# One core, sixteen batches: set-up loads in another order, batch 0's condition rows and the weight products in the score banks, waits at the first user, and a new order table

## What is computed

```python
ada = t_emb @ w_ada + b_ada                      # 16 rows of 1536; t_emb is cond_1024
sh_msa, sc_msa, g_msa, sh_mlp, sc_mlp, g_mlp = jnp.split(ada, 6, axis=-1)
xn = layer_norm(logmap0(x)); xm = expmap0(xn * (1 + sc_msa) + sh_msa)
q, k, v = heads(plin(xm, w_q, b_q)), ...         # 16 heads of 16
attn = softmax(qt @ kt / 4); attn_out = plin(from_heads(attn @ vt), w_o, b_o)
x = mobius_add(x, expmap0(g_msa * logmap0(attn_out)))
xm = expmap0(layer_norm(logmap0(x)) * (1 + sc_mlp) + sh_mlp)
ff = plin(plin(xm, w_f1, b_f1), w_f2, b_f2)      # no nonlinearity between the two
h = mobius_add(x, expmap0(g_mlp * logmap0(ff)))
y = x_in + attn_block(h)     # windows of 64, 64 latents, two sigmoid gates, w_out
out = y + moe(modulated(y, cond, weight))        # softmax, top 2 of 4, relu(x Wi + B A x) Wo
```

## Time and profile before

| | us |
|---|---|
| median of 3 runs | 1327.85 (1326.16 to 1328.44) |
| profiled execution | 1326.44 |
| its span | 1324.6 |
| TensorE busy | 1181.0 |
| VectorE busy | 906.8 |
| ScalarE busy | 711.2 |
| GpSimd busy | 214.9 |

### The profile page before, as it was taken

The page is one execution under the profiler, slowest core; times in us unless marked ns, Lnnn a source line. Parts: engine busy times, 40 slices in busy tenths (PEclk is TensorE's granted clock), DMA queues, the critical chain, the costliest instruction groups (busy, mean ns, idle before and its releaser), DMA issues.

```text
span 1324.6 us, 34251 instructions
## 1 busy us (share of the span) xinstructions
PE 1181.0 (89%) x13940; PEld 826.7 (62%) x13940; DVE 906.8 (68%) x3547; ACT 711.2 (54%) x1460; POOL 214.9 (16%) x176
## 2 busy tenths in 40 slices
PE   3867778989999999999999999999999989888776
PEld 1444445656666676767777676767676766666555
DVE  4557877877777797779777877697877784342412
ACT  0256676655567664575557655756575463333221
POOL 0301103012030220213021301122011220101101
PEclk8888898989999999999999999999999999999888
DMA  9210010001001010100000000000000000000000
GB/s 317 73 64 13 18 29 26 9 26 38 2 16 47 10 41 11 42 10 31 21 26 18 18 26 22 22 3 29 2 30 15 18 15 18 10 10 18 2 9 8
DMA packets 26974, 38.55 MB, mean 29 GB/s; under 512 B 3472, under 2 KB 21264, under 8 KB 26816
## 3 DMA queue, kind: packets, MB, share of 16 engines
q1 hardware_dynamic: 25472, 34.79, 8.3%
q10 hardware_dynamic: 1344, 1.57, 0.4%
HBM read 31.67 MB, written 4.29 MB: 27 GB/s over the span
## 4 chain that ended last, share of the span: by engine, by line
PE 68%; DVE 15%; ACT 12%; issue 3%; DMA 1%; POOL 0%; SPq 0%; DVEq 0%; POOLq 0%; ACTq 0%
PE psg L434 42%; PE psq L434 14%; PE pso L434 6%; PE psg L437 6%; ACT PQ L1337 6%; DVE TU L893 2%; DVE nm L896 1%; ACT QK L1337 1%; DVE ST L890 1%; DMA QK<-in_w_ada 1%; ACT M L1337 1%; ACT L1337 1%; DVE smf L890 1%; ACT JA L1348 1%; ACT OT L1340 1%
## 5 line engine op out<-in xcount | busy, mean ns | idle before, releaser
L1337 ACT ACTIVATE PQ<-psq 128x1280 f32<-128x1280 f32 (+2 forms) x144 | 215.5, 1496 | 102.2 <-PE psq L434 101.4
L1686 POOL TENSOR_TENSOR R<-R,rhoT 128x512 f32<-128x512 f32 x64 | 82.7, 1292 | 522.6 <-ACT R L1337 522.1
L434 PE MATMUL psg<-zT,WiT 128*128 128x256 f32 x512 | 126.0, 390 | 1.3 <-DVE R L893 1.3
L434 PE MATMUL pso<-PQ,Vg 128*32 128x256 f32 (+2 forms) x2048 | 116.8, 347 | 8.6 <-ACT PQ L1337 8.6
L434 PE MATMUL psq<-QK 32*128 32x128 f32 (+4 forms) x3328 | 123.2, 304 | 0.0
L434 PE MATMUL psg<-WoT,R 128*128 128x256 f32 x512 | 113.6, 379 | 0.0
L896 DVE TENSOR_REDUCE nm<-psq 128x16 f32<-128x2048 f32 (+1 forms) x48 | 92.8, 1933 | 26.1 <-PE psq L434 26.0
L434 PEld LDWEIGHTS psg<-zT,WiT 128*128 128x128 f32 x512 | 94.5, 194 | 16.5 <-issue 2.7
L434 PEld LDWEIGHTS psq<-QK 32*128 32x128 f32 (+1 forms) x3328 | 94.2, 166 | 16.4 <-issue 7.7
L434 PEld LDWEIGHTS psg<-WoT,R 128*128 128x128 f32 x512 | 95.9, 190 | 13.0 <-issue 0.5
L434 PE MATMUL psg<-wqkv,M 128*128 128x512 f32 (+1 forms) x256 | 97.8, 511 | 0.8 <-DVE ST L890 0.8
(11 more groups left out here) (223 smaller groups left out, 2360.3 us busy)
## 6 DMA issues: line engine op xcount, KB each, us to landing
bcA<-ada_rows SPq DMA_DIRECT2D x16, 384.0 KB, 3.4
...
QK<-NMT SPq DMA_DIRECT2D x128, 3.0 KB
...
```

Of the source, the lines that this page charges most:

```text
L434: return e.matmul(o, lhsT, rhs, start=start, stop=stop, skip_group_check=True)
L1337: return e.activation(o, i, func, **kw)
L1686: e.tensor_tensor(R4, R4, rhoT[:, :].unsqueeze(1).broadcast_to([128, 2, 256]), ALU.mult).then_inc(*pool_moe.mark(b, f"r{f}"))
```

## The change

The set-up loads come in another order: `w_ada` in four pieces, first those for columns 0 to 767, then the identity and `wqkv`, then the rest. The condition, both biases and `bqkv` are issued by ScalarE. One half of `w_ada` moves from `QK2` to `R2`, so that `w1T1` and `w21` no longer wait for the condition products. For batch 0 TensorE makes the first 768 condition values in all 128 partitions at once (the condition column broadcast as the stationary operand), VectorE adds the bias, which was loaded to 128 partitions, and writes `bcA[0]`. No DMA is in that path any more. The other rows go through the scratch as before. The weight products use banks 0 and 1 of `psq` instead of two `psg` banks, and are cut into pieces of two matmuls that the table places. Waits for loads that all stood in one place (`setup`, the end of `late`) stand at the first user. The norm factors are made for batch 0 alone, then 1 and 2, then 3. The table `ORDER` is new for all engines and over the whole program; a line of it is shown.

```diff
--- before
+++ after
@@ ORDER: the table of letters, one string of stages for each engine
-        "**n*qqqq**nhqhqqaqaaaan*aaaooohhoqaqqaaqaaaanaooohhoqaqqaaqaaaaaNooFFohhoaaaaaaaaooppppppomommnmNqqqFFql",
+        "AA*AAn*qqqq*******hhn**qqqqaanaaaaaaooohhqqqqaoaaaaaaanooohhqqqqaoaaaaaaNaooFFohhoaaaaaaaaooppppppnomqqq",
...
@@ where loads and signals are declared
-        wada = ST1.rearrange("p j n -> p (j n)"), QK2[0].rearrange("p e n -> p (e n)")[:, 0:1536]
+        wada = ST1.rearrange("p j n -> p (j n)"), R2.rearrange("p f n -> p (f n)")[:, 0:1536]
-        badaR = U[0][0:16, 0:768], U[1][0:16, 0:768]
+        bada = U[0][:, 0:768], U[1][0:16, 0:768]
-        pool_setup = sig("pool_setup", "ident", "identb", "zero", "ones")
+        pool_setup = sig("pool_setup", "zero", "ones", "ident", "identb")
-        quad = Banks([psq], dve_late.at(0, "ada3"))
-        po, pg = Banks([pso]), Banks(psg)
+        quad = Banks([psq], dve_ada.at(0, "a3"))
+        po, pg = Banks([pso], dve_ada.at(0, "a5")), Banks(psg)
-        units = [([0, 1], []), ([2, 3], []), ([], [0])]
+        units = [([0], []), ([1, 2], []), ([3], []), ([], [0])]
@@ TensorE
-            def setup():
+            def first(b, *names):
+                if not b:
+                    for k in names:
+                        w.wait_ge(*loads[k])
+            def ada(_):
+                yield
                 w.wait_ge(*loads["cond"])
                 for c in range(2):
-                    w.wait_ge(*loads[f"wada{c}"])
-                for j in range(3):
+                    w.wait_ge(*loads[f"wada{c}0"])
+                for j, n in ((0, 512), (1, 256)):
                     for c in range(2):
-                        last = mm(psq[0:16, j, :], condT[:, c, :], wada[c][:, 512 * j:512 * j + 512], c == 0, c == 1)
-                    last.then_inc(*pe_setup.mark(0, f"ada{j}"))
-                w.wait_ge(*pool_setup.at(0, "ones"))
-                for k in ("wqkv", "wo"):
-                    w.wait_ge(*loads[k])
+                        last = mm(psq[:, j, 0:n], condT[:, c, 0:1].broadcast_to([128, 128]), wada[c][:, 512 * j:512 * j + n],
+                                  c == 0, c == 1)
+                last.then_inc(*pe_ada.mark(0, "bc"))
+                for j, o in enumerate((psq[0:16, 2, :], psq[0:16, 3, :], pso[0:16, :])):
+                    yield
+                    if j:
+                        for c in range(2):
+                            w.wait_ge(*loads[f"wada{c}1"])
+                    for c in range(2):
+                        last = mm(o, condT[:, c, :], wada[c][:, 512 * j:512 * j + 512], c == 0, c == 1)
+                    last.then_inc(*pe_ada.mark(0, f"r{j}"))
             def late(_):
                 for ic in range(2):
-                    yield
-                    bank = take(pg, ("W", ic), act_late.at(0, f"W{ic}"))
-                    for k in ("w1T0", "w1T1", "w20", "w21"):
-                        w.wait_ge(*loads[k])
                     for f in range(8):
+                        if f % 2 == 0:
+                            yield
+                        if f == 0:
+                            w.wait_ge(*dve_ada.at(0, "c2"))
+                        w.wait_ge(*loads[f"w1T{f // 4}"])
+                        w.wait_ge(*loads[f"w2{f // 4}"])
                         v = wx[f // 4][:, f % 4, :]
-                        last = mm(bank[:, :], v[:, 128 * ic:128 * ic + 128], v, f == 0, f == 7)
+                        last = mm(psq[:, ic, :], v[:, 128 * ic:128 * ic + 128], v, f == 0, f == 7)
                     last.then_inc(*pe_late.mark(0, f"W{ic}"))
                 yield
                 bank = take(pg, ("b1w",), act_late.at(0, "b1x"))
...
-                yield
-                for k in ("wr", "wout", "w2c", "wrt", "wat0", "wat1", "wgkv", "WiT", "WoT"):
-                    w.wait_ge(*loads[k])
-                w.wait_ge(*dve_late.at(0, "Bst"))
-                w.wait_ge(*pool_late.at(0, "wgkv"))
-                w.wait_ge(*act_late.at(0, "b1b"))
...
+                    w.wait_ge(*pool_setup.at(0, "identb"))
+                    first(b, "wqkv")
+                        w.wait_ge(*act_late.at(0, "W1"))
+                first(b, "wo")
+                first(b, "wat0", "wat1")
+                        first(b, "WiT", "WoT")
...
@@ VectorE
+            def ada(_):
+                s = dve_ada
+                yield
+                w.wait_ge(*loads["bada0"])
+                w.wait_ge(*pe_ada.at(0, "bc"))
+                for k, i in enumerate((psq[:, 0, 0:256], psq[:, 0, 256:512], psq[:, 1, 0:256])):
+                    stt(bcA[0][:, k, :], i, float(k == 1), bada[0][:, 256 * k:256 * k + 256], ALU.add,
+                        ALU.add)().then_inc(*s.mark(0, f"c{k}"))
+                w.wait_ge(*loads["bada1"])
+                for j, i in enumerate((psq[0:16, 2, :], psq[0:16, 3, :], pso[0:16, :])):
+                    yield
+                    w.wait_ge(*pe_ada.at(0, f"r{j}"))
+                    for h in range(2):
+                        n, o = 2 * j + h, slice(256 * h, 256 * h + 256)
+                        k = 256 * (n % 3)
+                        stt(adaR[j][:, o], i[:, o], float(n in (1, 4)), bada[n // 3][0:16, k:k + 256], ALU.add,
+                            ALU.add)().then_inc(*s.mark(0, f"a{n}"))
             def late(_):
                 s = dve_late
...
-                yield
-                after(s)
-                for n, o in enumerate((adaR[0][:, 256:512], adaR[2][:, 0:256])):
-                    e.tensor_scalar(o, o, 1.0, None, ALU.add).then_inc(*s.mark(0, f"one{n}"))
                 yield
...
@@ ScalarE, the set-up
-                load(e, "bqkv", bqkv[:, :], A["bqkv"].partition_broadcast(128))
-                load(e, "bo", bo[:, :], A["b_o"].partition_broadcast(128))
+                load(e, "cond", condT[:, :, :], A["condT"].rearrange("(c p) b -> p c b", p=128))
+                load(e, "bada0", bada[0], A["b_ada"][0:768].partition_broadcast(128))
                 load(e, "w1T0", wx[0][:, :, 0:256], chunks("w1T")[:, 0:4])
                 load(e, "w20", wx[0][:, :, 256:512], chunks("w2")[:, 0:4])
+                load(e, "bqkv", bqkv[:, :], A["bqkv"].partition_broadcast(128))
+                load(e, "bada1", bada[1], A["b_ada"][768:1536].partition_broadcast(16))
+                load(e, "bo", bo[:, :], A["b_o"].partition_broadcast(128))
@@ GpSimd
-                return modulate(pool_norm, b, M1, bcA_in[b % 3].at(b // 3), bcA[b % 3], act_norm.at(b, "x1"))
+                rows_in = bcA_in[b % 3].at(b // 3 - (b % 3 == 0)) if b else dve_ada.at(0, "c2")
+                return modulate(pool_norm, b, M1, rows_in, bcA[b % 3], act_norm.at(b, "x1"))
@@ SyncE
-                load(e, "cond", condT[:, :, :], A["condT"].rearrange("(c p) b -> p c b", p=128))
                 for c in range(2):
-                    load(e, f"wada{c}", wada[c], chunks("w_ada")[:, c])
-                load(e, "bada0", badaR[0], A["b_ada"][0:768].partition_broadcast(16))
-                load(e, "bada1", badaR[1], A["b_ada"][768:1536].partition_broadcast(16))
+                    load(e, f"wada{c}0", wada[c][:, 0:768], chunks("w_ada")[:, c, 0:768])
+                load(e, "ident", ident0, A["ident"])
+                load(e, "wqkv", wqkv[:, :, :], chunks("wqkv"))
+                for c in range(2):
+                    load(e, f"wada{c}1", wada[c][:, 768:1536], chunks("w_ada")[:, c, 768:1536])
                 for _ in x_load(1):
                     pass
-                load(e, "ident", ident0, A["ident"])
-                load(e, "wqkv", wqkv[:, :, :], chunks("wqkv"))
-                load(e, "hsel", hsel[:, :], A["hsel"])
-                load(e, "wo", wo[:, :, :], chunks("w_o"))
-                for b in range(2, 4):
-                    for _ in x_load(b):
-                        pass
-                load(e, "b1c", b1c, A["b1c"])
-            def late(_):
-                chunks = lambda k: A[k].rearrange("(c p) n -> p c n", p=128)
-                yield
-                w.wait_ge(*pe_setup.at(0, "ada2"))
                 load(e, "w1T1", wx[1][:, :, 0:256], chunks("w1T")[:, 4:8])
                 load(e, "w21", wx[1][:, :, 256:512], chunks("w2")[:, 4:8])
-                yield
-                w.wait_ge(*dve_late.at(0, "one1"))
-                for j in range(3):
-                    e.dma_start(scratch[:, 512 * j:512 * j + 512], adaR[j]).then_inc(loads["ada"][0], 16)
+                load(e, "hsel", hsel[:, :], A["hsel"])
+                for _ in x_load(2):
+                    pass
+                load(e, "wo", wo[:, :, :], chunks("w_o"))
+                load(e, "b1c", b1c, A["b1c"])
+                for _ in x_load(3):
+                    pass
...
+            def ada(_):
+                for j, k in enumerate("AAB"):
+                    yield
+                    w.wait_ge(*dve_ada.at(0, f"a{2 * j + 1}"))
+                    e.dma_start(scratch[:, 512 * j:512 * j + 512], adaR[j]).then_inc(*loads[f"ada{k}"])
```

(6 more changed lines are left out.)

196 lines of the change are left out of this document (109 added, 87 removed).

## The result

The changed kernel takes 1293.7 us (median of 4 runs, 1292.49 to 1297.26) against 1327.01 (4 runs, 1326.06 to 1328.44) beside it. The ratio is 0.9753, 95% interval 0.973 to 0.9775, so it is 29.9 to 35.8 us faster. The forecast was 1293, and its range 1272 to 1318. The profiled execution took 1293.05 us, its span is 1291.3.

A forecast was written before the change was run, and what follows sets the result against it. TensorE was taken as the bound, busy 753.2 of 775 us mid-kernel, with gains only where it idles at the ends. Terms 14.7 + 2 + 0 + 10 + 8 off 1326.4 gave 1291.7, median 1293 us, range 1272 to 1318.

The forecast's parts named there:

- The start, term 14.7: Up to the first scores: these come at about 57 us in place of 71.7, 14.7 us earlier.
- Steps 1 to 6: Start, from first loads through weight products: batch 0's qkv at about 24.5 us in place of 49.97, products done at 47.3.
- the 10.5 of shared DMA engines: Start: condition values begin at 10.5 us if queues share DMA engines; separate queues would bring their 1 MB at 5 us.
- The two thin slacks: Start: heads ready at 42 to 44 us against 47, batch 1's condition values modulated at 44 against 48.
- step 7: End of the start: heads and transposes 1.3 us, bias and condition products 2.8, batch 1's qkv 5.3; first scores about 57.
- The early batches, term 2: From 71.7 to 157.7 us: 2 us gained, between -4 and +6.
- period of 28.8 us: Early batches: time from one attention output to the next, 28.8 us in place of 30.6.
- The middle, term 0: From 157.7 to 1075 us: no gain from the new order, between -15 and +15 us.
- The rival that the middle pays: From 300 to 1075 us: 0.45 us lost on each of 95 exponentials, 43 us more, 1336 us; chance 0.07.
- The tail, terms 10 and 8: 10 us gained from 1075 to 1271 (0 to 20), 8 in the last 53.6 us (3 to 11).
- The clock: Last 53.6 us: TensorE's higher clock gives 1.9 us in batch 15's mixing and 2 more in products up to 1300.
- sum of 34.7: Whole kernel: all terms together take 34.7 us off the profiled execution's 1326.4 us, giving 1291.7.

The follow-up runs named there:

- e4: Changed kernel with one piece of the next batch's qkv moved into TensorE's wait for VectorE's output tile, in batches 0 and 1: 1294.5 us.
- e2: Changed kernel's code and its order up to batch 0's attention output, then the order of the kernel before: 1317.57 us, ratio 0.9926 to the kernel before.
- e5: Changed kernel with the old set-up's waits for the ones and six loads put back ahead of TensorE's first weight product: 1306.93 us.
- e6: Changed kernel with the set-up loads of SyncE's queue in the order of the kernel before: 1297.62 us.
- e7: Changed kernel with batch 0's first condition rows written to the scratch and read back by DMA, as for other batches: 1320.88 us.
- e11: Changed kernel with the exponential of batch 0's first four heads put ahead of batch 2's two normed rows on ScalarE: 1296.84 us.
- e9: e2 with the changed kernel's relative order for everything left behind TensorE's last feed-forward: 1299.25 us.
- e3: Changed kernel with the order of the kernel before behind the last batch's feed-forward on each engine: 1330.12 us.

## Where the prediction was right and wrong

**The start, term 14.7: 12.4 in the profile.** Steps 1 to 6 came within a microsecond: TensorE's first matmul at 9.31 (forecast 10), batch 0's qkv at 24.46 (24.5), heads at 47.65 (47.3). That first matmul is near the 10.5 of shared DMA engines and far from the 5 of separate ones. The two thin slacks held: no wait stands before the heads, and batch 1's rows, issued at 38.03 with 3.4 us to landing, were back at about 41, as forecast. What failed are sizes in step 7. Its own terms behind 47.3 (1.3, 1.84, 2.8 and 5.3) add up to 58.5, not to 57; by them the term would have been 13.2. That 57 came near is partly luck: the products on the condition rows, put at 2.8, took 0.9 (51.37 to 52.26), which made up for the slip. And batch 1's qkv took 7.10 us and not 5.3. In e4, the same instructions up to there, it took 5.41, and the first scores came at 57.62 (in e2 at 57.34). The stretch from 52 to 59 us, first of the changed kernel:

```profile
52.00:56.00 4.00, 4.00 (x10) 0.58 0.00 0
56.00:59.00 3.00, 3.00 (x12) 0.99 0.00 0
```

and of e4:

```profile
52.00:56.00 4.00, 4.00 (x15) 1.00 0.00 0
56.00:59.00 3.00, 2.76 (x22) 1.00 0.00 0
```

So the term's number was right to 0.6 us for an execution without this dip, and the dip took 1.7. What makes up the term, by e5 to e7: this start needs both the waits at their users and rows that come early; the order of loads gives nothing that shows. Those two losses (13 and 27 us) are not parts of a sum; each alone undoes most of the start, and of e7's a part is the place of the writes in the queue. In the time e2 shows 9.8 of it, since the early batches give some back.

**The early batches, term 2: minus 3.7 in length** (86.0 before, 89.7 after), just at the forecast's lower edge of minus 4. The failed step is the period of 28.8 us. It came to 33.13 (83.99 to 117.12), against 30.62 before. The qkv block took 7.95 (forecast 7.6) and the chain 7.4 (7). The attention, from its scores at 91.94 to the last transposes of its output at 109.69, took 17.75 where I had 14.2. The rows of the changed kernel, TensorE and then ScalarE:

```profile
95.73 1.15 PE L435 MATMUL psq<-ST 32*128 32x256 f32 x16 [0.73 <-ACT PQ L1385]
...
106.63 1.37 PE L435 MATMUL pso<-PQ,Vg 128*32 128x256 f32 x16 [2.46 <-ACT PQ L1385]
```

```profile
92.09 1.09 ACT L1385 ACTIVATE M<-X,nmr,rln 128x256 f32<-128x256 f32 x2 [1.27 <-PE psg L435]
93.09 0.83 ACT L1385 ACTIVATE SQ<-U 128x768 f32<-128x768 f32 x1
93.82 1.86 ACT L1385 ACTIVATE PQ<-psq 128x2048 f32<-128x2048 f32 x1
...
104.60 0.20 ACT L1385 ACTIVATE sf<-sf 128x2 f32<-128x2 f32 x1 [2.15 <-DVE sf L918]
104.71 1.86 ACT L1385 ACTIVATE PQ<-psq 128x2048 f32<-128x2048 f32 x1
```

I had counted four exponentials and their handoffs, as if ScalarE did nothing else. But the fourth stands in its queue behind an operation of 0.20 us on `sf` that waits 2.15 us for VectorE: the four periods took 14.7 us (91.94 to 106.63) and not 13.2. The end, put at 1 us, took 3.1 (to 109.69), because besides the last values it holds another batch's transposes (`ident,M`), and the transposes ran at a granted clock of 0.51 (107.9 to 110.75). With the qkv pieces gathered ahead of the attention, TensorE has little beside it. Before, qkv pieces lay between the scores, as in this stretch of the kernel before:

```profile
102.12 2.85 PE L434 MATMUL psg<-wqkv,M 128*128 128x256 f32 x8
104.90 1.15 PE L434 MATMUL psq<-ST 32*128 32x256 f32 x16
```

In e4 and e11 a wait of the early batches was shortened, and time was lost again a few steps on.

**The middle, term 0:** 3.5 us of idle time lost between 300 and the last `WG,mT`, inside plus or minus 15. The rival that the middle pays was right in sign: TensorE's waits of `psq` for `PQ` went from 3.1 us in 4 to 8.5 in 10. At 95 exponentials that is 0.06 us each, far under the 0.39 from which it would have decided.

**The tail, terms 10 and 8:** of these 18 us 14 were idle time and 3.9 clock. Idle time fell by 20.0, and e9 puts the worth of the tail's own order at 18.3 us. The waits named in the forecast (`rho`, `LW`, the mixing run alone) are the ones that went, and behind the last `ident,XR` nothing did (12.7 and 12.8 us idle), as forecast. So the forecast 18 is near what the tail's own order is worth. What failed is the step before it: the sum put the middle at 0 beside the tail, as if the two were independent. They are one arrangement. With the old tail the new early and middle order loses 12.5 us (e3 against e2). With the new tail it loses nothing: it pays 7.2 us of idle time before 1055 (2.5 and 4.7), and the 16 expert steps it holds back take 5.5 us out of the tail's waits again (16.2 to 10.7).

**The clock.** The forecast had 3.9 us for it, at the end. Outside the start TensorE's busy time fell by 9.5 us (5.9 in all, and 3.7 more at the start, where products were added). That is what made up for the early batches. As runs of one order differ by several us in busy time, how much of it belongs to the change isn't settled. That the sum of 34.7 meets a measured 33.4 (1326.44 less 1293.05) is partly such cancelling, and so partly luck.
